# A vision tower on one core: the second half of the class values moved into the last attention, with new orders at the end

## The reference

```python
h = tokens(x)                                   # [64, 65, 128], token 0 is the class token
q, k, v = split_heads(norm(h) @ W.T + b)        # 8 heads of 16
attn = softmax(einsum('bhnd,bhmd->bhnm', relu(q), relu(k)) / (relu(k).sum(-1) + eps))
h = h + einsum('bhnm,bhmd->bhnd', attn, v) @ Wo.T + bo
flat = layernorm(norm(h))
h = h + swiglu(flat @ shared_in.T) @ shared_out.T + shared_b \
      + sum_e comb[:, e] * (swiglu(flat @ expert_in.T) @ expert_out[e].T) + cnt @ expert_bias
```

## Time and profile before

| | us |
|---|---|
| three timed executions | 466.17, 464.65, 463.91 |
| their median | 464.65 |
| the profiled execution, whole | 468.48 |
| its span | 466.7 |
| mean granted clock of TensorE | 0.977 |
| TensorE busy | 441.4 (95%) |
| VectorE busy | 307.6 (66%) |
| ScalarE busy | 190.3 (41%) |
| GpSimd busy | 181.2 (39%) |

### The profile page before, as it was taken

One profiled execution on the slowest core, in us unless ns is written; L12 is line 12 of the kernel. 1 busy time (PEld: TensorE's weight loads), 2 busy tenths in 40 slices (PEclk: granted clock), 3 DMA queues, 4 the chain that ended last, 5 costly groups with the idle time before them and its releaser, 6 DMA issues.

```text
span 466.7 us, 6933 instructions
## 1 busy us (share of the span) xinstructions
PE 441.4 (95%) x2313; PEld 311.2 (67%) x2313; DVE 307.6 (66%) x896; ACT 190.3 (41%) x358; POOL 181.2 (39%) x220
## 2 busy tenths in 40 slices
PE   6969999899999999999999999999999999999982
PEld 2335455656786687667865788668856888887651
DVE  0151476486867876696659674868588877777665
ACT  1015523752276326641563238422752186321520
POOL 7112721222175306531652246304732256134453
PEclk9989999999999999999999999999999997899988
DMA  8998655135004520263007400530000000000000
GB/s 330 389 402 313 199 171 182 64 114 168 36 1 130 185 68 1 67 207 108 0 10 244 129 0 2 188 126 0 2 24 0 2 0 1 2 23 1 0 25 25
DMA packets 16451, 45.96 MB, mean 98 GB/s; under 512 B 1904, under 2 KB 7584, under 8 KB 16416
## 3 DMA queue, kind: packets, MB, share of 16 engines
q1 hardware_dynamic: 14704, 43.50, 27.8%
q10 hardware_dynamic: 1712, 2.02, 1.2%
HBM read 43.39 MB, written 2.13 MB: 98 GB/s over the span
## 4 chain that ended last, share of the span: by engine, by line
PE 77%; DVE 8%; DMA 4%; issue 4%; POOL 3%; ACT 2%; ACTq 1%; POOLq 0%; DVEq 0%
PE acc L483 22%; PE O L577 6%; PE B L469 6%; DMA bq_row<-in_bq_row 4%; PE scores L547 2%; PE scores L703 2%; PE C L703 2%; PE C L704 2%; PE C L705 2%; PE scores L705 2%; PE scores L704 2%; PE B L526 2%; PE C L635 2%; PE B L512 1%; PE C L665 1%
## 5 line engine op out<-in xcount | busy, mean ns | idle before, releaser
L483 PE MATMUL acc<-x_main,w_patch 128*128 128x512 f32 x288 | 141.4, 614 | 5.8 <-DMA w_patch<-in_w_patch 4.1
L483 PEld LDWEIGHTS acc<-x_main,w_patch 128*128 128x128 f32 x288 | 51.3, 195 | 48.3 <-issue 38.6
L1885 POOL TENSOR_TENSOR prod<-prod 128x512 f32<-128x512 f32 x31 | 39.9, 1286 | 27.9 <-DVE q_nat L1325 10.7
L993 ACT ACTIVATE probs_t<-B 128x512 f32<-128x512 f32 x32 | 19.1, 597 | 54.7 <-PE B L469 54.7
L577 PEld LDWEIGHTS O<-v_bd,probs_t 128*128 128x128 f32 x256 | 33.5, 200 | 10.4 <-issue 7.7
L1878 POOL TENSOR_TENSOR hidden_lo<-silu,hidden_hi 128x512 fp32r<-128x512 f32 x16 | 20.3, 1271 | 40.8 <-ACT hidden_hi L993 40.8
L577 PE MATMUL O<-v_bd,probs_t 128*128 128x64 f32 x256 | 33.2, 280 | 0.0
L1820 POOL TENSOR_TENSOR rstd<-var,neg_half 128x4 f32<-128x4 f32 x8 | 8.1, 1019 | 50.8 <-DVE var L1282 50.8
L1365 DVE TENSOR_TENSOR attn_patch<-O,row_rec 64x256 f32<-64x256 f32 x32 | 13.5, 422 | 21.5 <-PE O L577 20.8
L993 ACT ACTIVATE probs<-shift 128x512 f32<-128x512 f32 x32 | 20.1, 628 | 18.0 <-DVE shift L1338 16.8
L703 PE MATMUL scores<-w_eout_hi,hidden_hi 128*128 128x512 f32 x64 | 27.3, 426 | 0.0
(11 more groups left out here) (334 smaller groups left out, 1012.6 us busy)
## 6 DMA issues: line engine op xcount, KB each, us to landing
x_main<-in_x_main SPq DMA_DIRECT2D x40, 768.0 KB, 4.3
x_main<-in_x_main SPq DMA_DIRECT2D x8, 512.0 KB, 4.1
x_main<-in_x_main SPq DMA_DIRECT2D x8, 256.0 KB, 3.3
x_tail<-in_x_tail SPq DMA_DIRECT2D x8, 224.0 KB, 4.9
out_tokens<-y_out SPq DMA_DIRECT2D x14, 128.0 KB, 2.6
prod<-in_w_eout SPq DMA_DIRECT2D x2, 512.0 KB, 14.7
w_patch<-in_w_patch ACTq DMA_DIRECT2D x5, 192.0 KB, 10.1
silu<-in_w_in SPq DMA_DIRECT2D x2, 256.0 KB, 13.6
```

What stands on the lines that cost most here:

```text
L483: last = mm(acc[:, :], w_patch[:, j, :], x_main[:, j, :], start=(j == 0), stop=False)
L993: return nc.scalar.activation(dst, src, func, **kw)
L1885: q.tensor_tensor(p[r, 0, :], p[r, 0, :], p[r, 1, :], ALU.add).then_inc(tree1_done.sem, 1)
```

## The change

The same matmuls are done, in another order and partly into other banks.

1. Input products: `ffn_in(L-1, 3)` writes banks `O` and `B1`, and `score(L, 0)` stands ahead of it instead of behind it. On VectorE `row_maxes(L, 0)` stands ahead of `hidden_mul(L-1, 3)`.
2. Class values: all of the first 11 pairs stand behind `score(L, 1)`. The 21 others, so far spread over the expert products behind `out_proj(L)`, move into the last attention: 7 pairs ahead of `prob_v(L, 2)`, 14 behind `prob_v(L, 3)`. Their lower rows go into bank `scores[0]`, and ScalarE copies them out from there. `class_softmax(1)`, `class_probs(1)` and its copy move ahead to match. `class_own` is one VectorE instruction shorter.
3. Behind `out_proj(L)` the expert products 1, 2 and 3 now follow each other, then `z_transpose(L)`, 4 and 5, and the rest is moved up accordingly. On VectorE `weights(L-1)` stands ahead of `residual(L, 1)`, `weigh(L-1, 0)` and `shared_add(L-1)` ahead of `norm2_scale(L)`, `weigh(L-1, 7)` ahead of `class_residual`.
4. The end: `expert(L, 4)` and `expert(L, 5)` stand ahead of the class tokens' `shared_t` and expert products. GpSimd does `expert_sum(L, 2)` ahead of `class_sum`. VectorE has `class_output` last and `output(L, 3)` behind `weigh(L, 7)`. SyncE stores the class tokens last.

```diff
         def ffn_banks(g, k):
...
+            if g == GROUPS - 2 and k == 3:
+                return O, B1
...
             def expert(g, u, rows):
...
+                elif u == 1 and g == GROUPS - 2:
+                    pe.wait_ge(tval_done.sem, 2)
...
             def class_values(first, end):
-                need(pe, tpr_done, 1 if end > IMAGES // 4 else 0)
                 if first >= EARLY:
-                    need(pe, o1_done, GROUPS - 1)
+                    need(pe, tpr_done, 1)
+                    need(pe, sub_done, GROUPS - 1, 3)
                 else:
+                    need(pe, tpr_done, 0)
                     pe.wait_ge(tmax_step.sem, 8)
+                    need(pe, hid_done, GROUPS - 2)
                 for pair in range(first, end):
-                    for b2, bank, col in ((0, acc, pair * HEADS), (1, O, pair * HEADS + (128 if pair < EARLY else 0))):
+                    for b2, bank, col in ((0, acc, pair * HEADS), (1, O if pair < EARLY else scores[:, 0, :], pair * HEADS)):
...
             ffn_in(L - 1, 2, TOK)
+            score(L, 0)
             ffn_in(L - 1, 3, TOK)
-            class_values(0, 5)
-            score(L, 0)
             score(L, 1)
-            class_values(5, EARLY)
+            class_values(0, EARLY)
...
+            class_probs(1)
             prob_transpose(L, 3)
             counts(L - 1, TILES, 128)
+            class_values(EARLY, 18)
             prob_v(L, 2)
             prob_v(L, 3)
+            class_values(18, IMAGES // 2)
...
             def class_own():
-                dve.wait_ge(tval_done.sem, 1)
...
+                dve.wait_ge(tval_done.sem, 2)
...
         VectorE, behind the last attention
+            weights(L - 1, TILES, 128)
             residual(L, 1)
             norm2(L, h2[1], TILES, 128)
-            weights(L - 1, TILES, 128)
+            weigh(L - 1, 0, 128)
+            shared_add(L - 1, h2[0], TILES, 128)
             norm2_scale(L, h2[1], TILES, 128)
-            shared_add(L - 1, h2[0], TILES, 128)
-            weigh(L - 1, 0, 128)
...
         VectorE, the end
-            class_output()
-            output(L, TILES - 1, 128)
             weigh(L, 6, 128)
             last_tile(0)
             weigh(L, 7, 128)
+            output(L, TILES - 1, 128)
             last_tile(1)
+            class_output()
...
         GpSimd, the end
+            expert_sum(L, 2, 128)
             class_sum()
-            expert_sum(L, 2, 128)
```

99 lines of the change are left out of this document (52 added, 47 removed).

## The result

| | us, median (lowest to highest), executions | mean granted clock |
|---|---|---|
| kernel before, in the same comparison | 465.41 (463.91 to 468.53), 4 | |
| changed kernel | 472.38 (472.04 to 472.53), 4 | .970 in each |
| ratio | 1.0134, interval 1.0098 to 1.0169 | |
| profiled execution after | 472.41, span 470.6 | .970 |
| profiled execution before | 468.48, span 466.7 | .977 |

Predicted were 463.6 us and a range of 460.0 to 467.2. Profile against profile the span grew by 3.9 us, where -1.0 had been forecast; median against median it grew by 7.0 us.

What follows compares the result with a forecast made beforehand. TensorE was taken as the bound until 458 us, with 8.7 us behind its last matmul. Unchanged-clock terms +2.0, clock +3.4 and end -6.4 gave -1.0 on 464.65: 463.6 us, range 460.0 to 467.2 (the sum's own 461.5 to 465.8).

Steps and rivals of the forecast that it cites:

- rival in which the thin stretches join: Last attention: clock not back when the 7 pairs begin, whole stretch at half clock, 8.1 us instead of 3.4; 468.4; chance 0.15.
- opening: Opening of the last attention: TensorE stands some 0.7 us, where it stood 0.50 later on; +0.2 us, ends -0.3 and +0.8.
- end (2.1 idle, 1.7 clock, 2.6 order): Kernel's end: experts 4 and 5 fill the count wait, half clock goes, last work reordered; -6.4 us, ends -7.0 and -4.0.
- hidden products of L behind the experts' order: VectorE falls behind TensorE, about 1.2 us idle before the shared product of L, where 0.41; +0.7 us, ends 0 and 1.3.
- late pairs, their cover and their clock: 21 pairs moved into last attention: less switching -0.3, exposed chain to L's normalised input +1.4, further half clock +3.4 us.
- fall in the new thin stretch: Last attention, beginning between 404 and 412 us: further half-clock stretch of 6.8 us, costing 3.4 us, ends 0 and 8.1.
- first rival: Last attention: only idle time lowers the clock, so the 7 us thin stretch costs nothing extra; 460.2 us; chance 0.18.
- waits of 1.1 and 0.3 us: TensorE waits 1.1 us for shared_add before expert 3, 0.3 for low part of z before L's input products; together 1.4.
- old count wait: TensorE's 2.11 us idle before the class tokens' shared product; experts 4 and 5 fill it, -2.1 us.
- from profile to median: Base of the sum: timed median 3.8 us below the profiled execution, difference carried over unchanged; 464.65 - 1.0 = 463.6 us.
- third rival: Kernel's end: fall at 448.71 seldom in timed runs, or stores or class_sum set the end; gives 4.0, 466.1 us; chance 0.15.
- second rival: Last attention: half clock holds for more than about 14 us, costing 8.1 us instead of 3.4; 468.4 us; chance 0.15.

Runs made afterwards that it cites:

- experts-only kernel: Kernel before with the change's opening, end and order of group L-1's experts, the 21 late class value pairs left between the experts: 464.29 us, ratio 0.9980.

## Why profile and median differ: the same kernel runs at several clocks

Each comparison executes the kernel before again, so over the study 113 executions of it have both a time and a mean granted clock: .973 to .991 and 462.4 to 470.6 us, median .984 and 466.3. The times follow the clock (correlation -0.92): a straight line through them is 3.4 us longer for each 0.01 less clock, and leaves a scatter of 0.6 us. The profiled execution (.977, 468.48) lies near the low end of the clock. In what follows, "at the same clock" means a kernel's distance from this line at its own clock (time = 801.9 - 341.2 x clock); at .970 and below the line is extended. It is a fit to one kernel and not a mechanism: in the other kernels with ten or more executions the same fit gives 2.2 to 4.3 us for each 0.01, so the split of a difference into clock and rest is rough.

**The kernel before, profiled again.**

> The kernel before, profiled once more, to see which half-clock stretches an execution other than the first (clock .977, 468.5 us, stretches at 32.3, 390.7, 448.7 us and the end) has. Clock theory for the 3.8 us between that profile and the median: a profile at .984 or more lacks one or two of the short stretches (32.3 and 448.7 us) and is 2 to 5 us shorter. Rival (something else, as DMA or another engine, makes the first profile long): the same stretches, another time.

Measured: 463.7 us, span 461.8, clock .991. Its clock line and windows:

```profile
PEclk9999999999999999999999999999999999999987
```

```profile
385.80:396.10 10.30, 9.44 (x110) 8.09 (x111) 8.59 (x16) 7.49 (x19) 7.00 (x9) 1.00 0.01 2
396.10:443.10 47.00, 43.71 (x284) 34.15 (x284) 36.13 (x120) 16.86 (x35) 18.89 (x26) 1.00 0.04 11
443.15:446.56 3.41, 3.41 (x9) 2.27 (x9) 1.52 (x5) 0.17 (x1) 3.17 (x5) 0.50 0.09 22
```

The fall at 32.3 us is missing, as expected; but the other one that is gone is the long one of the last attention, not the short one before the end. The 16 products of 64 columns in the attention that took 414 ns each in the earlier trace rows take 275 ns here:

```profile
L577 PE MATMUL O<-v_bd,probs_t 128*128 128x64 f32 x16 | 2.0, 275 | 0.0
```

So a thin stretch of the same instructions falls in one execution and not in another. What decides that in an execution no row shows. The Trainium skill, "TensorE: Matmul & The Clock Gate", section "What's actually happening", says that the chip's view of TensorE's activity runs free of the kernel, so that one kernel measures differently from run to run; the spread here fits that, but no run here shows the cause.

**The changed kernel again.**

> The changed kernel itself, again, beside the others on this chip. Its four executions so far all held a mean granted clock of .970 and 472.0 to 472.5 us, while 52 of the kernel before spread over .973 to .991 and 463.5 to 469.7 us, 3.2 us for each 0.01 of clock. If the change's second thin stretch falls whatever the execution: median 472.4 within 0.6 us, clock .966 to .972. Rival (the four were alike by chance and the change has the spread of the kernel before): median 469.5 to 471.5 us, clocks up to .98.

Measured: 471.60 us (470.23 to 472.98, 6 executions), clocks .970, .970, .973, .973, .973, .977; before beside it 466.08; ratio 1.0114 (1.0082 to 1.0147). This is between the two expectations, 0.2 us below the first and 0.1 above the rival's range. The rival's wide spread is not there: all ten executions of the change lie at .970 to .977, where only the slow end of the 113 lies. In this profile the first stretches lie differently (3.41 us at half clock from 390.05, full clock to 400.29, then 13.65 us in one piece). That is the shape of the rival in which the thin stretches join; its total is the same 17.1 us as 10.24 + 6.83 in the first profile.

At the same clock the change is only 1.5 to 1.8 us above the kernel before. Of the 6.1 us between the medians 472.4 and 466.3, the larger part, 4.8 us by the line (.984 to .970), goes with the clock; by the slopes of the other kernels it would be 3 to 6 us.

## The experiments: the change taken apart

**The end alone.** The kernel before with this, and VectorE's and GpSimd's order of the end to match:

```
-            shared_t(GROUPS, IMAGES)
             expert(L, 4, 128)
+            expert(L, 5, 128)
+            shared_t(GROUPS, IMAGES)
             expert(GROUPS, 0, IMAGES)
             expert(GROUPS, 1, IMAGES)
             shared_natural(GROUPS, 1, IMAGES)
-            expert(L, 5, 128)
```

> The kernel before with part 4 (the end) alone: expert products 4 and 5 ahead of the class tokens' shared product, the last tile sum ahead of class_sum, class_output and its store last. The end theory: 2.1 us of idle time, 1.7 us of half clock and 1.2 to 2.6 us of order go, so 4.0 to 6.4 us less than the kernel before (465.4): 459.0 to 461.4, no half clock near 449. Rival (the changed kernel's end gained nothing, its loss is less because something else gained): within 1 us of the kernel before.

Measured: 462.15 us (12 executions), ratio 0.9924 (0.9891 to 0.9956), before 465.66; clock .986. The end gains 3.5 us, 3.3 at the same clock. It is a gain, but less than the 4.0 to 6.4 us expected. The profile has no half clock near 449, so that sign holds. TensorE's waits behind 385 us no longer hold the 2.1 us for the counts:

```profile
PE B L469 <- ACT exp_cls L993: 0.5, 1, 0.5
PE B L665 <- DVE silu L1492: 0.4, 1, 0.4
PE B L592 <- ACT attn_t L993: 0.2, 1, 0.2
```

**The change without the end**, the reverse of this edit on the changed kernel:

> The changed kernel with part 4 (the end) undone. The end theory: 4.0 to 6.4 us more than the changed kernel's 472.4, so 476.4 to 478.8. Rival: within 1 us of 472.4.

Measured: 477.22 us (474.60 to 479.25, 4 executions), ratio 1.0246 (1.0182 to 1.0310). This is inside the end theory's range. Without its end the change costs 11.6 us; the end is worth 4.8 to 5.6 us there, by the two measurements of the change. In both settings it gains, and in both less than the 6.4 us of the forecast.

**The opening and the end.** The end alone, and the opening's edits on all engines:

```
             ffn_in(L - 1, 2, TOK)
+            score(L, 0)
             ffn_in(L - 1, 3, TOK)
-            class_values(0, 5)
-            score(L, 0)
             score(L, 1)
-            class_values(5, EARLY)
+            class_values(0, EARLY)
```

> The kernel before with two parts of the change: the end (as in the run with the end alone, 462.15 us there) and the opening (first score between the input products, the 11 early class values' pairs together, the orders of ScalarE, VectorE and GpSimd that go with it). The late class values and the experts stay where they were. Opening theory (opening is neutral, +0.2 forecast, first transposes 0.6 us later in the changed kernel's trace): 462.1 to 463.0 us, mean granted clock .983 to .989, one half-clock stretch before 400 us. Rival (11 pairs in a row make the thin opening longer at half clock, and part of the loss sits here): 464 us or more, clock .980 or less, half-clock time before 400 us of 13 us or more.

Measured: 462.51 us (6 executions), ratio 0.9904 (0.9867 to 0.9940), clock .986. The opening costs 0.4 us against the end alone (0.2 forecast), within what these runs can tell from nothing.

**The experts' order as well.** The 21 late pairs still stand between the experts:

```
-            z_transpose(L)
             expert(L - 1, 3, 128)
             class_values(23, IMAGES // 2)
+            z_transpose(L)
+            expert(L - 1, 4, 128)
+            expert(L - 1, 5, 128)
             ffn_in(L, 0, TOK)
-            expert(L - 1, 4, 128)
             gates(L, TILES, 128)
-            expert(L - 1, 5, 128)
...
```

> The kernel before with the opening and the end (462.51 us there) and, in addition, the change's order of the group before last's experts: expert products 4 and 5 ahead of the first input product, 6 and 7 one place earlier, and VectorE's products 4 to 7 likewise. The 21 late class value pairs stay between the experts. This splits the loss of about 10 us between the opening-and-end kernel and the change in two. If the experts' order brings the waits (the class values' output product waits for a hidden product that stands behind two more expert products on VectorE): 463.6 to 465.0 us, a wait of 1 to 2.5 us at that product in the profile, the rest of the loss is the class values' place. Rival (the waits are there only because the 21 pairs no longer stand between the experts as cover): 462.2 to 463.2 us and no wait over 0.5 us.

Measured: 464.29 us (12 executions), ratio 0.9980 (0.9945 to 1.0014), clock .985. That is 1.8 us more than with the opening and the end by the medians and 3.5 by the two ratios, so the size is known only to within some 2 us. The wait is there, so it comes from the order, not from missing cover:

```profile
PE B L763 <- DVE silu L1503: 2.4, 1, 2.4
```

What remains from here to the change, 7.3 us to the 471.60 of its second measurement and 8.1 to the first, is the place of the late class values, with the orders of VectorE and ScalarE that belong to it (`shared_add` ahead of `norm2_scale` among them; these were not taken apart): 2.4 to 2.7 us at the same clock, the rest goes with the clock, from .985 to .970 or .973.

**The parts together:** end -3.5, opening +0.4, experts' order +1.8, the values' place +7.3 give +6.0 us. Each kernel of this chain holds the one before it, so the sum has to come out, but for the drift between comparisons; it is no test of the parts. The second measurement of the change has +5.5 against the kernel before, the first +7.0.

## The experiments: is it the thin stretch?

**The 14 pairs behind dense work.** The same matmuls, in the changed kernel, behind the shared product and expert 0:

```
             prob_v(L, 3)
-            class_values(18, IMAGES // 2)
             shared_t(L - 1, TOK, (1,))
             expert(L - 1, 0, 128)
+            class_values(18, IMAGES // 2)
```

> The changed kernel with the 14 late pairs of class values behind the shared product and expert product 0 instead of ahead of them: 2.5 us of 512-column matmuls then stand between the two thin pieces; the amount of work is the same. The clock theory (the second thin stretch lowers TensorE's clock, 6.8 us at half clock, 3.4 us lost): no or a shorter half-clock stretch behind 404 us, 2 to 3.4 us less than the changed kernel, 469.0 to 470.4. The chain theory (the loss is the waits for VectorE that the class values used to cover): unchanged within 0.7 us, 471.7 to 473.1.

Measured: 469.63 us (12 executions), ratio 1.0087 (1.0059 to 1.0116), clock .979 instead of .970 to .973. This is 2.0 to 2.7 us faster and inside the clock theory's range. At the same clock it stands at +1.3 us, the change at +1.5 to +1.8: nearly all of the gain is clock. In its profile the 14 pairs begin at 409.62, behind 512-column matmuls, and the clock stays up beneath them. But it had fallen before, at 401.35, among the 7 pairs, and this profile lacks the fall from 390 us:

```profile
401.35:408.18 6.83, 6.83 (x32) 5.68 (x31) 4.06 (x13) 0.00 (x0) 1.03 (x3) 0.50 0.16 41
408.18:415.00 6.82, 6.57 (x78) 5.77 (x77) 1.43 (x8) 2.13 (x4) 0.00 (x0) 1.00 0.00 1
```

One profile is not enough here. In that of the run with both causes mended, below, the pairs stand in the same place, from 409.07, and the clock falls among them, at 411.75:

```profile
411.75:418.58 6.83, 6.83 (x35) 6.18 (x34) 1.47 (x5) 2.39 (x4) 0.00 (x0) 0.50 0.00 0
```

So the dense work between makes the fall rarer, by the clocks of the executions; it does not rule it out.

**The 14 pairs left out.**

```
-            class_values(18, IMAGES // 2)
+            class_values(IMAGES // 2, IMAGES // 2)
```

> The changed kernel with the 14 class value pairs that stand ahead of out_proj, between prob_v and the second half of the shared product, left out of the computation (28 matmuls and their weight loads). They took 4.5 us in the profile after, largely at half clock; 7 such pairs at full clock took 1.76 us, so 14 would be 3.5 us. Work theory (they cost their own time only): 467.9 to 468.9 us, the half-clock stretch at 408 us still there. Clock theory (their thin matmuls are what halves the clock from 408.5 us): the stretch is gone, the work behind them in it runs full too, and the time is 466.4 to 467.8 us.

Measured: 465.67 us (10 executions), clock .977; 6.7 us less than the change. At full clock these pairs take about 3.2 us (409.62 to 412.85 in the profile of the run before this one), and 4.3 us is what they took with the fall in them (406.53 to 410.84 in the profile after). Time they did not occupy went as well, more than the clock theory's range allowed for: -4.1 us at the same clock, -2.6 from the clock. The profile has no half clock at 408.5; the window there:

```profile
401.50:408.40 6.90, 6.90 (x63) 5.91 (x62) 4.22 (x14) 2.27 (x5) 1.03 (x3) 1.00 0.17 40
```

**All profiles together.** Half-clock stretches that begin between 384 and 415 us, added up, in each of the 17 profiles of this study:

| late pairs | profiles | half clock, us |
|---|---|---|
| in the attention, as in the change | 6 | 13.7 (two), 17.1 (four) |
| the 14 behind dense work | 2 | 6.8 and 17.0 |
| the 14 left out | 1 | 10.2 |
| all 21 or more behind out_proj | 8 | 0 (three), 3.4 (one), 10.2 (four) |

With the late pairs in the attention every profile has more half clock than any without them. That is the main evidence for the thin stretch.

**The experts put back, the values left in their new place.** Experts 4 to 7 of L - 1 stand among the input products again, as in the kernel before, on TensorE and VectorE:

```
             z_transpose(L)
-            expert(L - 1, 4, 128)
-            expert(L - 1, 5, 128)
             ffn_in(L, 0, TOK)
+            expert(L - 1, 4, 128)
             gates(L, TILES, 128)
+            expert(L - 1, 5, 128)
...
```

> The changed kernel with experts 4 to 7 of group L-1 back among the input products of L (each one place later, as in the kernel before, and VectorE's weighings with them); the class values stay in the attention. The chain theory: TensorE now waits about 3.0 us for z ahead of the first input product (expert products 4 and 5 no longer cover it), but the 2.3 us wait ahead of class_out goes, and with it the half-clock stretch of 3.4 us behind it (1.7 us): 472.4 + 2.8 - 2.3 - 1.7 = 471.2. Rival (an idle time of 3 us lowers the clock in its turn): 472.9 or more.

Measured: 471.57 us (4 executions), ratio 1.0125 (1.0070 to 1.0180). The time is as expected. The wait at class_out is gone and a longer one stands before the first input product, since nothing covers the chain to the low part of z any more; what the rival had named, half clock behind that wait, is there too, 3.4 us of it from 426.8:

```profile
425.39 0.47 PE L645 MATMUL B<-z_hi,w_in_hi 128*128 128x512 f32 x1 [2.98 <-POOL z_lo L1884]
```

At the same clock it is 1.2 to 1.4 us worse than the change; its clock was better (median .9775). With the values gone, the experts are needed as cover, and either order leaves a wait of 2.3 to 3.0 us.

**Hidden product ahead of expert products 6 and 7 on VectorE:**

```
             hidden_mul(L, 1, TOK)
-            weigh(L - 1, 6, 128)
             hidden_mul(L, 2, TOK)
+            weigh(L - 1, 6, 128)
             weigh(L - 1, 7, 128)
```

> The changed kernel with one move on VectorE: the products for experts 6 and 7 of the group before stand behind the third hidden product, not in front of the second and third gap. The class values' output product waited 2.34 us for that hidden product (L765). Wait theory: the wait shrinks by one or two expert products, 0.7 to 1.4 us, to 471.0 to 471.7 us; with the clock theory added, a shorter idle stretch ahead of 439 us no longer halves the clock for 3.41 us, and the time is 469.3 to 470.3 us. Rival (other VectorE work sets the hidden product's time): 472.4 us, no change.

Measured: 469.65 us (10 executions), ratio 1.0082 (1.0052 to 1.0111). The wait shrank, by 0.6 us:

```profile
436.10 0.40 PE L765 MATMUL B<-w_attn,x_main 128*64 128x128 f32 x2 [1.75 <-DVE silu L1506]
```

The profile has no half-clock stretch near 439 any more, and the mean clock of the executions is .975 to .982. At the same clock nothing changed (+1.8). So the 2.0 to 2.7 us go with the clock, as expected of a shorter idle stretch there; of the wait itself hardly anything came back. The profiles agree: behind each of the seven waits of 2.3 to 3.0 us in this part (at class_out, or at the first input product in the run above) a half-clock stretch of 3.4 us begins within 1.7 us, and behind none of the four waits of 1.2 to 1.8 us. Behind the wait of 2.1 us for the counts one begins within 1.6 us in both profiles of the kernel before.

## The experiments: what makes the wait at class_out

Open was whether the overlap with GpSimd makes this wait or only the number of expert products ahead of the hidden product. One move on VectorE, in three kernels:

```
             hidden_mul(L, 0, TOK)
-            weigh(L - 1, 4, 128)
             logits(L, TILES, 128)
             choose_shift(L, TILES, 128)
-            weigh(L - 1, 5, 128)
             choose_top(L, TILES, 128)
+            weigh(L - 1, 4, 128)
             hidden_mul(L, 1, TOK)
-            weigh(L - 1, 6, 128)
+            weigh(L - 1, 5, 128)
             hidden_mul(L, 2, TOK)
+            weigh(L - 1, 6, 128)
```

**In the experts-only kernel.**

> The experts-only kernel (464.29 us there; 462.51 without the experts' order) with one move on VectorE: expert products 4 and 5 of the group before last stand behind the choice of experts and not inside it, 6 behind the third hidden product. Overlap theory (GpSimd's sum of products 4 and 5, 1.29 us long, ran beside the choice and held the multiplication of the choice at 1.29 us instead of 0.29 and the addition at 0.48 instead of 0.19): both are back at 0.29 and 0.19, the wait at the class values' output product shrinks from 2.4 us to 1.0 or less, and the time is 462.4 to 463.5 us. Rival (only the number of expert products ahead of the third hidden product counts; it goes from three to two, 0.6 us): wait 1.7 us or more, 463.6 to 464.3 us.

Measured: 464.54 us (12 executions), ratio 0.9956 (0.9929 to 0.9984); clock .985 like the kernel without the move. The operations and the wait go the way of the overlap theory, but not all the way to its 0.29 and 1.0 us:

```profile
423.75 0.44 DVE L1456 TENSOR_TENSOR e_ge<-e_ge,const 128x128 f32<-128x128 f32 x1
...
424.95 0.19 DVE L1461 TENSOR_TENSOR e_top<-e_row,e_col 128x32 f32<-128x32 f32 x1
```

```profile
428.24 0.40 PE L763 MATMUL B<-w_attn,x_main 128*64 128x128 f32 x2 [1.22 <-DVE silu L1503]
431.56 1.13 PE L676 MATMUL B<-hidden,w_sout 128*128 128x512 f32 x2 [0.90 <-DVE silu L1503]
```

The choice's first operation (g_sel), which took 0.48 us, now takes 0.96 beside an earlier sum of GpSimd:

```profile
421.71 0.96 DVE L1434 TENSOR_TENSOR g_sel<-g_logit 128x4 f32<-128x4 f32 x1
```

So of 1.6 us of overlap in three operations 0.9 are left. The edit also takes one expert product (0.6 us) from the front of the hidden product, as the rival said, and 0.7 + 0.6 is a little over the 1.1 us by which the wait shrank.

By the time neither range holds: 464.54 against 464.29 us, 0.6 better at the same clock. The wait of 2.36 became 1.22, but TensorE now waits 0.90 us before the shared product, for the last hidden product, which stands behind the expert products that were put off. The rows fit a stretch bound by VectorE, in which the move shifts its work and takes away only what the overlap cost; of this 0.6 us at most arrives.

**In the change.**

> The changed kernel (472.38 and 471.60 us) with the same move on VectorE. Overlap theory: the wait of 2.34 us shrinks to 1.0 or less, and with it the half-clock stretch near 439 goes: 468.3 to 469.8 us, at the same clock 0.6 to 1.5 us better than the change. Rival (number of products alone): as the run with the hidden product moved ahead, 469.6 us or more, nothing at the same clock.

Measured: 470.07 us (10 executions), ratio 1.0078 (1.0050 to 1.0105), clock .979. The wait is 1.2 us, the half clock near 439 is gone, and 1.5 to 2.3 us are gained, all of it with the clock; at the same clock it stays where it was (+2.0). In time that is the rival's outcome. For the wait, this run and the one with the hidden product moved ahead can be compared: both have two expert products ahead of the hidden product. There the multiplication of the choice still takes 1.28 us and the wait is 1.75; here it takes 0.43 and the wait is 1.22. So 0.5 us of the wait are shown to be the overlap, and 0.6 the one product.

**In the change with the 14 pairs behind dense work.**

> The change with the 14 class value pairs behind the shared product and expert 0 (469.63 us) and the same move on VectorE. If the thin stretch and the overlap are the two causes and separate: 467.0 to 468.4 us. Rival (they are one cause, and mending either gives it all): 469.2 to 470.0 us. It can't come to the 462.5 us of the kernel without the move of the late values, since the wait of 1.1 us before expert 3 stays.

Measured: 468.79 us (465.38 to 472.56, 12 executions), ratio 1.0026 (0.9994 to 1.0058), clock .976. It is 0.8 us under the kernel with the pairs moved alone, 1.2 at the same clock, and lies between the two expectations; 0.8 us is less than these runs can tell from nothing. Mending both suspected causes brings 2.8 to 3.6 of the change's loss back. It does not bring back the 462.5 us of the kernel without the late pairs' move and the experts' order.

## The experiments: the opposite, and a version that beats both

**The opposite of the change.** In the tail kernel (the better version below) all 32 pairs stand behind out_proj, none in the attention:

```
             score(L, 1)
-            class_values(0, EARLY)
...
             expert(L - 1, 1, 128)
-            class_values(EARLY, 17)
+            class_values(0, EARLY)
             expert(L - 1, 2, 128)
-            class_values(17, 23)
+            class_values(EARLY, 21)
...
```

> The tail kernel (461.65 us there) with the 11 early class value pairs taken out of the last attention as well: all 32 pairs stand between the experts behind out_proj, none in the attention; they stay in TensorE's own bank pair and ScalarE's copy of them falls away. It is the opposite of the change: thin matmuls out of the attention instead of more of them in. Clock theory (tiny matmuls in the attention are what brings the half-clock stretch of 390 us in some executions): mean granted clock up to .988 or more in most executions, median 459.5 to 461.0 us. Rival (the early pairs fill time in which TensorE would wait for the exponentials, so taking them out leaves idle time there and their 2.4 us are now on the path): 462.5 to 465 us, clock no better.

Measured: 462.81 us (460.41 to 469.43, 12 executions), ratio 0.9942 (0.9900 to 0.9983). The rival holds for the time: the pairs had filled a wait for the exponentials, and this is what stands there now:

```profile
388.44 0.66 PE L469 MATMUL B<-const,probs 128*128 128x128 f32 x4 [1.49 <-ACT exp_cls L998]
```

The clock became wider, not better: five executions at .991 to .995 (460.4 to 462.2 us) and five at .972 to .979 (466.4 to 469.4). Taking the tiny matmuls out of the attention did not do away with the low executions; none of them was profiled, so where their clock fell is not shown. At the same clock the kernel lost 1.7 us.

**A better version.** The opening and the end as above, and two edits at the very end:

```
-            sp.wait_ge(ycls_done.sem, 1)
-            sp.dma_start(out[:, 0, :], y_cls[0:IMAGES, 0:D]).then_inc(stored.sem, 16)
+            act.wait_ge(ycls_done.sem, 1)
+            act.dma_start(out[:, 0, :], y_cls[0:IMAGES, 0:D]).then_inc(stored.sem, 16)
...
-            weigh(L, 7, 128)
             output(L, TILES - 1, 128)
+            weigh(L, 7, 128)
```

> The same kernel as the opening-and-end one, and two edits at the very end: the class rows' store is issued from ScalarE's queue and not as the fifth on SyncE's, and the last group's output for tiles 0 to 2 stands ahead of the last expert product on VectorE. In the profile after the five last stores are issued in a row, 2.54 us for four and 0.59 us for the fifth (SPq L451, L460), from the moment tiles 0 to 2 are ready. If the issue of stores sets the end: 0.6 to 1.2 us under the opening-and-end kernel. Rival (the landing of the last tile's stores sets it, whoever issues the class rows): within 0.3 us of it.

Measured: 461.65 us (12 executions), ratio 0.9895 (0.9864 to 0.9927), before 466.18. Against the opening-and-end kernel it is 0.9 us less by the medians and 0.4 at the same clock, both inside the scatter: whether its two edits help is not settled. That the end, with or without opening and tail, beats the kernel before by 0.8 to 1.0% and the change by 2% is.

## Why the prediction was wrong, step by step

| step | forecast, us | measured, us | by |
|---|---|---|---|
| opening | +0.2 | +0.4 | opening and end against end alone |
| end (2.1 idle, 1.7 clock, 2.6 order) | -6.4 | -3.5 (-4.8 in the change) | end alone; change without it |
| hidden products of L behind the experts' order | +0.7 | +1.8 | experts' order |
| late pairs, their cover and their clock | -0.3 + 1.4 + 3.4 = +4.5 | +7.3 | the change against experts' order |

These are medians, and they sum to +6.0 where -1.0 was forecast: 7.0 us. The other 1.7 of the miss of 8.7 us is the base, 464.65, against 466.3 in 113 executions. The profiles can be read by themselves instead: there the change cost +3.9 where -1.0 was forecast, 4.9 us, and the other 3.8 is the difference between profile and median. Of the 4.9, by rows and as an estimate, 1.1 is the wait at class_out (2.34 for 1.2), 1.7 the half clock behind it (half of 3.42), 1.3 the tail (7.5 for 6.2) and 0.4 the opening (transposes 0.6 us later for 0.2). The two ways must not be added.

**What held.** The fall in the new thin stretch came where it was forecast, for 6.83 us against 6.8, and with TensorE busy ahead of it. Leaving the pairs out took it away, and with dense work between it was rarer. So the first rival, that the clock holds where TensorE has no idle time, is out, and with it the rule of the Trainium skill, "TensorE: Matmul & The Clock Gate", section "Why this matters for your kernels", as a full account: no idle gap is recorded ahead of 408.51, and the clock fell. The waits of 1.1 and 0.3 us were there as worked out. The old count wait and the fall at 449 were gone.

**The step "from profile to median" failed, and is the largest single term.** "I carry the difference over" took 3.8 us for a property that both kernels share. It is a property of one execution: the profiled one happened to be at .977, and 113 others spread over 8 us with their clock. The changed kernel's ten executions had none that could bring its median below its profile; the thin part of its last attention fell in both its profiles and in those of its four variants with the same place of the pairs. A part of the 3.8 us was also the small number of runs: their median, 464.65, is 1.7 us under that of the 113.

**The end was mis-sized by 2.9 us.** All its terms were read from one execution that held the fall at 448.71 and an 8.7 us tail. Median against median, the clock term is not 1.7 us: the end alone runs at .986 and the kernel before at .984, which is 0.7 us by the line, though both profiles of the kernel before have the short fall there and that of the end alone has not. And the tail is 7.5 us in the change, not 6.2, by the collision of VectorE's addition with class_sum (0.9 us) and the fifth issue (0.6). The third rival, -4.0 us for the end, named the stores and class_sum, and was given 0.15.

**The experts' order was mis-sized by 1.1 us, at the wrong place.** The step compared VectorE's work with TensorE's up to the shared product of L and found a wait of 1.2 us there. But class_out stands ahead of the last input product and waits for a hidden product too; so the delay shows one product earlier and twice as large, 2.34 us, and it brought a half-clock stretch at 439.23 behind it. The order alone shows the same wait (2.4). What the step did not look at is when GpSimd runs: of the 2.34 us, 1.6 (1.28, 0.49 and 0.49 less 0.29, 0.19 and 0.18) are the choice held up by GpSimd. With 0.7 of it moved away and one product fewer ahead the wait fell to 1.2 us, though little of that reached the end. The rule could have been seen at work before: in the trace of the kernel before, an addition of 64x128 with both inputs in SBUF took 1.28 us beside a GpSimd sum of 1.27 us that had started 0.13 earlier.

```profile
457.26 1.28 DVE L1552 TENSOR_TENSOR x_main<-x_main 64x128 f32<-64x128 f32 x1 [1.11 <-POOL x_main L1902]
```

**The values' place was mis-sized by 2.8 us.** Here the mechanism, a fall in the new thin stretch, was right. The clock term was taken for one execution of each kind; in the medians the clock goes from .985 to .970 or .973, some 4 to 5 us by the line, because every profile of the change has the falls and one of the two of the kernel before has not. How much of these is the stretch at 408.51 and how much that at 439.23, the runs tell only roughly: dense work ahead of the first gave 2.0 to 2.7 us, shortening the wait ahead of the second 1.5 to 2.7.

**The range and the second rival.** The stated range of the sum, 461.5 to 465.8, is not what its ends give: added up with the base 464.65 they reach from 457.9 to 472.5, mostly by the clock (0 to 8.1) and the end (-7.0 to -4.0), and 472.4 lies just inside. The second rival was to hold above 14 us of half clock in the last attention, but the forecast itself had 10.24 + 6.8 = 17.0, so that sign could not tell them apart. The change has 17.1 us in both profiles, in one piece of 13.65 and one of 3.41 in the second; the rival's price, 468.4, was still 4 us short.

**Left open:** why the same instructions fall in one execution and not in the next, and why the median of the change was 472.38 in one comparison and 471.60 in the other.

## What to carry to other kernels

Before a profile is used as a sum's base, look at the clock of several executions: where time follows clock, terms must be read for a typical execution, and a stretch near the edge of falling is an expected cost in both kernels, not a fixed one. Tiny matmuls were cheap fill here where a wait stood; gathered into a stretch that already was thin they cost the clock of the work near it, and 512-column work between them made that rarer without ruling it out. When work that covered a chain is moved, follow each consumer of that chain in the engine's order, small products such as class_out included, not only the large ones.

## What the runs showed of the hardware that was not expected

- The granted clock fell to 1.2 GHz behind 6.82 us in which TensorE was recorded as busy without a gap (90 matmuls, nearly all of 8 to 128 columns); with 512-column matmuls ahead of them the same 14 pairs ran at 2.4 GHz throughout in one profile and fell to 1.2 GHz near their end in another.
- It also fell within 1.7 us behind each of seven waits of TensorE of 2.3 to 3.0 us near the last input products, and behind none of four of 1.2 to 1.8 us.
- One kernel's executions spread from 462.4 to 470.6 us with mean clocks of .991 to .973; 3.4 us for each 0.01. That is 0.37 us for each us at half clock (0.01 of a span of 464 us is 9.3 us at half), less than the 0.5 that work twice as slow would lose. Why is not shown; part of the half clock lies behind TensorE's last matmul (from 466.5 us in the profile after), where it can cost nothing.
- VectorE's operations with two inputs in SBUF grew by up to 1.0 us where they started just behind a GpSimd operation. At the end it was an addition of 128x128, 1.23 us in place of 0.29, in the change and in the tail kernel, where both started 0.2 us apart:

```profile
453.34 1.30 POOL L1908 TENSOR_TENSOR x_main<-x_main 64x512 f32<-64x512 f32 x1
453.56 1.23 DVE L1548 TENSOR_TENSOR x_main<-x_main,prod 128x128 f32<-128x128 f32 x1
...
456.82 0.29 DVE L1548 TENSOR_TENSOR x_main<-x_main,prod 128x128 f32<-128x128 f32 x1
```
